# Global attention: the value products of two key blocks in one run, in every second block

## The reference

```python
aperture = jax.nn.sigmoid(x @ Wa + ba)
expression = jax.nn.sigmoid(x @ We + be)
inner = (x @ Wi).reshape(Bb, Tt, Hh, dh).transpose(0, 2, 1, 3)
outer = (x @ Wo).reshape(Bb, Tt, Hh, dh).transpose(0, 2, 1, 3)
alignment = jnp.einsum('bhqd,bhkd->bhqk', inner, outer) / scale
attn_align = jax.nn.softmax(alignment, axis=-1)
attn = attn_align * aperture.transpose(0, 2, 1)[..., :, None] * expression.transpose(0, 2, 1)[..., None, :]
attn = attn / (attn.sum(axis=-1, keepdims=True) + 1e-08)
v = (x @ Wv).reshape(Bb, Tt, Hh, dh).transpose(0, 2, 1, 3)
converged = jnp.einsum('bhqk,bhkd->bhqd', attn, v)
```

## Time and profile before

| | us |
|---|---|
| median of 3 executions | 5294.77 (5292.79 to 5297.17) |
| the profiled execution | 5297.09 |
| its span in the trace | 5294.9 |
| PE busy | 4984.7 |
| DVE busy | 4059.0 |
| ACT busy | 2803.4 |
| POOL busy | 1137.2 |

### The profile page before, as it was taken

The page is one execution under the profiler, slowest core; times in us unless marked ns, Lnnn a source line. Parts: engine busy times, 40 slices in busy tenths (PEclk is TensorE's granted clock), DMA queues, the critical chain, the costliest instruction groups (busy, mean ns, idle before and its releaser), DMA issues.

```text
span 5294.9 us, 83713 instructions
## 1 busy us (share of the span) xinstructions
PE 4984.7 (94%) x29772; PEld 3073.3 (58%) x29772; DVE 4059.0 (77%) x10911; ACT 2803.4 (53%) x5521; POOL 1137.2 (21%) x1469
## 2 busy tenths in 40 slices
PE   3899999999999989999999999999999999999998
PEld 1233333333333326777777777777777777777776
DVE  3788878788887856778777777777778777777876
ACT  1566666666666654555454455545445554555544
POOL 2112021120211002222222222222222222222221
PEclk7899999999999999999999999999999999999999
DMA  5333233233323220000000000000000001000000
GB/s 114 89 62 69 42 69 60 49 63 61 64 41 72 42 47 6 8 7 12 8 25 16 7 8 10 9 26 11 12 7 8 10 9 30 7 12 7 8 10 6
DMA packets 165058, 161.76 MB, mean 31 GB/s; under 512 B 26180, under 2 KB 157080, under 8 KB 164512
## 3 DMA queue, kind: packets, MB, share of 16 engines
q1 hardware_dynamic: 164640, 156.42, 14.4%
HBM read 111.48 MB, written 44.09 MB: 29 GB/s over the span
## 4 chain that ended last, share of the span: by engine, by line
PE 56%; DVE 23%; ACT 7%; issue 6%; SPq 3%; DMA 3%; POOL 2%; POOLq 0%; DVEq 0%; ACTq 0%
PE psum L630 7%; PE psum L798 7%; PE psum L773 7%; PE psum L648 6%; PE psum L660 6%; PE psum L837 5%; PE psum L846 4%; DVE big_s L1353 4%; PE psum L821 4%; DVE mx L1150 3%; ACT big_s L996 2%; ACT pT_s L1019 2%; PE psum L613 2%; DMA stack<-parts_d 2%; PE psum L810 2%
## 5 line engine op out<-in xcount | busy, mean ns | idle before, releaser
L1150 DVE TENSOR_REDUCE mx<-psum 128x1 f32<-128x512 f32 x2048 | 1335.0, 686 | 317.6 <-PE psum L630 312.6
L935 ACT ACTIVATE pr<-psum 128x1024 f32<-128x1024 f32 x1024 | 1021.6, 1023 | 640.3 <-PE psum L648 629.2
L996 ACT ACTIVATE big_s<-big_s,mxl_s 128x256 f32<-128x256 f32 x1024 | 507.5, 496 | 621.8 <-DVE mxl_s L1361 621.8
L630 PE MATMUL psum<-stack 96*128 96x512 bf16 x2048 | 727.7, 389 | 67.3 <-DMA stack<-parts_d 25.0
L798 PE MATMUL psum<-wqkv_sb,uT_s 128*128 128x512 f32 x1536 | 748.3, 610 | 1.0 <-DVE uT_s L1314 1.0
L866 PEld LDWEIGHTS psum<-hlT_s,w_sb 128*114 128x114 f32 (+1 forms) x6144 | 683.9, 178 | 103.0 <-ACT hlT_s L1011 55.4
L866 PE MATMUL psum<-hlT_s,w_sb 128*114 128x128 f32 (+1 forms) x6144 | 715.8, 275 | 24.4 <-DVE hlT_s L1398 22.0
L630 PEld LDWEIGHTS psum<-stack 96*128 96x128 bf16 x2048 | 196.5, 96 | 754.4 <-DVE mx L1150 285.4
L648 PE MATMUL psum<-stack 99*128 99x512 bf16 x2048 | 614.4, 381 | 14.5 <-DMA stack<-mrow 13.6
L660 PE MATMUL psum<-pr,vg 128*32 128x512 f32 x4096 | 547.2, 606 | 0.4 <-ACT pr L935 0.4
L821 PE MATMUL psum<-kT_s,qz_s 128*128 128x256 f32 x2048 | 503.6, 384 | 6.0 <-DVE kT_s L1342 5.9
(11 more groups left out here) (165 smaller groups left out, 6537.1 us busy)
## 6 DMA issues: line engine op xcount, KB each, us to landing
stack<-parts_d SPq DMA_DIRECT2D x384, 128.0 KB, 5.9
parts_d<-parts SPq DMA_DIRECT2D x64, 384.0 KB, 2.8
hn<-in_x SPq DMA_DIRECT2D x8, 1024.0 KB, 9.9
xr<-in_x SPq DMA_DIRECT2D x8, 1024.0 KB, 5.4
x_d<-xr SPq DMA_DIRECT2D x8, 1024.0 KB, 9.6
tab<-tab_d SPq DMA_DIRECT2D x32, 256.0 KB, 2.6
mask_s<-in_mask SPq DMA_DIRECT2D x64, 128.0 KB, 2.4
out_x<-o_s SPq DMA_DIRECT2D x64, 128.0 KB, 1.7
```

The source lines that it names most:

```text
L630: pe.matmul(psum[:, to, :], stack[0:KS, g % 2, 0, u % 2, h, a * P:(a + 1) * P], stack[0:KS, g % 2, 1, kh, h, :], start=True, stop=True).th ...
L935: act.activation(pr[:, e % 2, 2 * pair:2 * pair + 2, :], psum[:, 2 * pair:2 * pair + 2, :], ACT.Exp, scale=DH ** -0.5).then_inc(s_exp, 1)
L996: ins = act.activation(w["big"][:, h, :], w["big"][:, h, :], ACT.Exp, bias=w["mx"][:, h:h + 1], accum_out=w["z"][:, h:h + 1])
L1150: dve.tensor_reduce(mx[:, u % 2, m, kh:kh + 1], psum[:, src, :], AX.X, ALU.max).then_inc(s_max, 1)
```

## The change

`pr` gets a third buffer, chosen by the running number of the step over all batches, modulo 3. In an even step PE leaves the value products out: the score `q0 + 3` stands directly behind `q0 + 2`. In an odd step PE does the value products of `e - 1` and of `e`, one after the other. `s_pv` counts pairs of runs, and those who wait for it use half the number: ACT's exponentials of step `e` wait for the pair that holds the step three before. DVE, POOL and SP do what they did, in the same order.

```diff
...
             o_sb = tmp("o_sb", [P, HALF])
             stack = tmp("stack", [P, 2, 2, NH, G, HALF], BF16)
             vg = tmp("vg", [P, 2, NT, G, VW])
-            pr = tmp("pr", [P, 2, G, HALF])
+            pr = tmp("pr", [P, 3, G, HALF])
             vt = tmp("vt", [P, NT, D])
             zt = tmp("zt", [P, NT, NEA])
             ze = tmp("ze", [P, NT, H])
...
                         pe.wait_ge(s_osb, b * NU + u)
                 for h in range(G):
                     mm = pe.matmul(psum[h * VW:(h + 1) * VW, ACC, :], vg[:, (u // 2) % 2, kc, h, :],
-                                   pr[:, e % 2, h, :], start=(kc == 0), stop=(kc == NT - 1))
-                mm.then_inc(s_pv, 1)
+                                   pr[:, (b * NE + e) % 3, h, :], start=(kc == 0), stop=(kc == NT - 1))
+                if e % 2:
+                    mm.then_inc(s_pv, 1)
 
             def heads(b, u, to):
 
...
                     next_score(q0 + 2)
                     if job:
                         late(b, *job, bank(place[job]))
-                    pv(b, e, first)
+                    if e % 2:
+                        pv(b, e - 1, first)
+                        pv(b, e, first)
                     next_score(q0 + 3)
 
             for at, (kind, n) in enumerate(first_ring):
...
                 act.activation(zt[:], zt[:], ACT.Exp, scale=-1.0).then_inc(s_z_exp, 1)
 
             def take_result(b, u):
-                act.wait_ge(s_pv, b * NE + (u * NT + NT))
+                act.wait_ge(s_pv, (b * NE + u * NT + NT) // 2)
                 if u > 0:
                     act.wait_ge(s_oT_ps, b * NU + u)
                 act.activation(o_sb[:], psum[:, ACC, :], ACT.Copy).then_inc(s_osb, 1)
 
             def exp(b, e, pair, first):
                 act.wait_ge(s_st_ps, b * (NU * 16) + (2 * e + pair + 1))
-                if e >= 2 or (e > 0 and not first):
-                    act.wait_ge(s_pv, b * NE + (e - 1))
-                act.activation(pr[:, e % 2, 2 * pair:2 * pair + 2, :], psum[:, 2 * pair:2 * pair + 2, :],
+                if b * NE + e >= 3:
+                    act.wait_ge(s_pv, (b * NE + e - 3) // 2 + 1)
+                act.activation(pr[:, (b * NE + e) % 3, 2 * pair:2 * pair + 2, :], psum[:, 2 * pair:2 * pair + 2, :],
                                ACT.Exp, scale=DH ** -0.5).then_inc(s_exp, 1)
 
             def batch(b, first, last):
...
                     gp.wait_ge(s_v, b * NT + NT)
                     gp.nop(nofuse=True)
                 if g > 1 or prev:
-                    gp.wait_ge(s_pv, b * NE + (g - 1) * 16)
+                    gp.wait_ge(s_pv, (b * NE + (g - 1) * 16) // 2)
                     gp.nop(nofuse=True)
                 e = ze[:, :, G * g:G * (g + 1)]
                 gp.tensor_tensor(vg[:, g % 2, :, :, 0:DH], vt[:, :, G * DH * g:G * DH * (g + 1)].rearrange("p t (h i) -> p t h i", i=DH),
```

## The result

| | us |
|---|---|
| changed kernel, median of 4 | 5428.94 (5425.17 to 5435.30) |
| kernel before, median of 4 on the same chip | 5293.78 (5291.55 to 5297.17) |
| ratio | 1.0256, 95% interval 1.0238 to 1.0274 |
| span of the profiled execution | 5425.9 (before 5294.9) |

A forecast was written before the change was run, and what follows sets the result against it. PE sets the pace, DVE having 18% to spare. A batch: 20.8 + 9.3 - 6.2 - 6.1 = +17.8 us; six inner batches +107, first and last +32, DMAs -8: +131, so 5426 us, range 5385 to 5460.

The forecast's parts named there:

- Entry and exit: PE's value products: 0.09 us to enter and 0.10 to leave a run; joining saves 0.19 a pair, 49 us in all.
- Even steps: PE reaches the fourth score before DVE or ACT releases the job's bank; waits of 20.8 us a batch.
- rows 5 and 8: Profile timelines before the change, read for even-step waits: 0.67 us with heads (row 5), 1.59 with v (row 8).
- Odd steps: Eight scores come faster than DVE reduces: 18 pairs lose 5.9 us, four with the transpose 3.4, together 9.3 a batch.
- The walk of the pair without jobs: Scores A to H followed through a jobless pair: 5.89 us against 5.68 before, some 0.33 of it wait.
- DMAs: PE's 9.6 us of waits for stack<-parts_d shrink as steps lengthen; 8 us counted back, 0 to 10 possible.
- The clock: PE's granted clock left unchanged, as the added waits are shorter than its longest present one, 1.9 us.
- Only entries and exits: Rival: only the entries and exits of value-product runs change, no added waits; -49 us, 5246; chance 4%.
- Odd steps don't wait: Rival: even steps wait but reductions keep up in odd ones; -74 us, 5352; chance 8%.
- Every pair bound by the release chain: Rival: each of 256 pairs loses a full 0.90 us to bank releases; 230 us, 5525; chance 3%.
- The runs don't join: Rival: the second run's matmuls wait for the first run's end, same bank; +25 us, 5451; chance 8%.
- Theory 2: Rival explanation posed for the experiments: the loss comes from ACT, its three buffers and its waits; no chance given.

The follow-up runs named there:

- e8: Changed kernel with the score q0 + 3 of an even step put behind the first two st matmuls of the odd step; 5426.2 us, ratio 1.0252.
- e6: Changed kernel with all eight v jobs in odd steps, none in an even one; 5428.2 us, ratio 1.0251.
- e1: Kernel before with the third buffer of exponentials alone, value products still in every step; 5292.5 us, ratio 0.9997.
- e5: Changed kernel with DVE doing proj's rest and v's logits one reduction earlier, so the job's bank is released sooner; 5432.2 us, ratio 1.0260.
- e2: Kernel before with DVE's reductions for the maxima reading 64 of 512 columns, so the maxima are wrong; 5219.5 us, ratio 0.9857.
- e3: Changed kernel with the same short reductions as e2, 64 of 512 columns; 5282.6 us, ratio 0.9976.
- e4: Kernel before with DVE doing proj's rest and v's logits one reduction earlier, so the job's bank is released sooner; 5278.0 us, ratio 0.9963.
- e10: e5 with the five splits of the maxima each one maximum earlier on DVE as well; 5403.2 us, ratio 1.0208.

## Why the prediction was right, point by point

- **Entry and exit.** A pair of joined runs takes 1.86 us where I had counted 1.90, so the second run costs 0.86, nearly the lower bound of 0.85. A pair costs 0.09 + 1.86 = 1.95 where it cost 2 x 1.09 = 2.18: 0.23 gained, 59 us in all, where 49 were counted. So between two runs of one mode nothing is paid here. The rule that a change of tiling mode drains the engine (the Trainium skill, TensorEngine Tiling (Array Packing), Key Properties) agrees with this trace. But the value products are f32 and the scores bf16, and no run tells what the mode costs from what the type does.
- **Even steps.** The waits read from rows 5 and 8 came out to 0.01 us (0.67 and 1.58). The list has 105.5 us of idle PE for `rest`, `zt`, `cv` and `xr` in 6.5 batches, 16.2 a batch. With the matmul's tail, 0.15 us in both places shown (0.67 against 0.52, 1.58 against 1.43), for each of the 18 waits it is 18.9, of 19.0 counted for these kinds.
- **Odd steps.** The walk of the pair without jobs gave 5.89, and 5.85 was measured. The 0.04 are the join. One sentence of the walk is wrong: 5.89 - 5.68 + 0.19 are 0.40 us of wait, 0.33 of them in the odd half and 0.07 in the even one, not 0.33 in both. The sum used the right parts. e8 and e6 show a side that the walk had in it but the text didn't stress: in pairs with heads DVE's chain over the whole pair is the limit, and a wait that is taken away in one place comes back in another.
- **DMAs.** 8 us had been counted back. The waits for `stack<-parts_d` fell from 9.6 us in 7.0 batches to 3.1 in 6.5, some 7 us over all eight. How sure this is can't be said: e1 does its work in the order of the kernel before and had 6.1.
- **The clock.** I left it as it is because no new wait would be longer than one that PE had. Its cost was small in the changed kernel, three falls of at most 1.7 us each, but the reason doesn't hold: in e5 it fell 14 times, and none of PE's waits from 300 to 1900 us was over 1.1 us.
- **Sum.** +131.0 us of span against +131 forecast. By ACT's last copy in each batch the first batch took 14.2 us more (16 counted), the six inner ones 102.2 (107, less their share of the 8 for the DMAs), the last 13.3 (16), and what follows it 1.4 (nothing). Part of the agreement is luck: the join gave 10 us more than counted, the first and last batch cost 4.5 less, and something of that size was counted too small elsewhere (the three falls of the clock, and smaller waits for `mx` that my classes of steps had at 0.07).
- **Rivals.** "Only entries and exits" had its gain right and its silence on the cover wrong. "Odd steps don't wait" fell with the pair of steps 16 and 17. "Every pair bound by the release chain" is right for pairs like 44 and 45 and wrong for the mean, which is 17.0 us over 32 pairs, 0.53 a pair against 0.90. "The runs don't join" fell with the 1.86 us. Theory 2 fell, as the cause of most of the loss, with e1 and with the 63 us between e2 and e3. The halved counts of `s_pv` weren't tried alone; the changed kernel's list has no wait of PE for ACT or POOL that they could have caused.

What I expected of the experiments was less exact than the forecast: e4 brought 17 of 30 us, e5 none of 20, e8 3 of 15, and e6 none that its runs can tell. In each a second wait stood close behind the first, and in e5 and e8 the clock fell more often besides. That the falls of the clock account for e5's missing gain is read from its trace and borne out by e10, where the longest of the waits is gone and the falls with it; it wasn't tried by itself.

## What to carry to other kernels

When work on the bound engine is moved to save its own switches, ask first what other engines did while it ran there: here 0.23 us of entry and exit were bought with 1.09 us of cover, in front of a bank whose release stood up to 1.6 us away. How long an answer takes can be read before the change, as the releasing operation's end less the time at which the waiting engine would be free; a mean of 18% free time says nothing about it. And with a ring of few banks look at the order in which the reader releases them: two reorderings of DVE's list gained 0.6% in the kernel before, without any work saved.

## What was not expected of the hardware

The granted clock fell for some microseconds in the middle of a dense stage, although none of PE's waits from 300 to 1900 us was over 1.1 us. In e5 the stretch before such a fall had PE busy for 1.77 of 3.40 us, in two waits of 0.55 and 1.08 us. After it the joined run took 2.72 us instead of 1.92. It happened at the same two places of each batch, 14 times, and with the longer of the two waits shortened (e10) it happened no more. So short waits that come close together can cost more than their own length; how close they must be, no run here shows.
